# A decoder layer on one core: cross attention in another order, with a new passage into it and new ends behind it

## The reference

```python
x = x + attention(layernorm(x), W_qkv)                     # one head of 128, causal
x = x + cross_attention(layernorm(x), ctx, ctx, mask, ...) # 16 heads of 8, biases on q, k, v and output
x = x + ffn(layernorm(x), w_gate, w_up, w_down)            # 128 -> 384 -> 128, quantised
```

## Time and profile before

| | us |
|---|---|
| median of 3 runs | 374.4 |
| lowest, highest | 369.46, 376.76 |
| profiled execution | 369.51 |
| its span, first to last instruction | 367.7 |

### The profile page before, as it was taken

One profiled execution on the slowest core, in us unless ns is written; L12 is line 12 of the kernel. 1 busy time (PEld: TensorE's weight loads), 2 busy tenths in 40 slices (PEclk: granted clock), 3 DMA queues, 4 the chain that ended last, 5 costly groups with the idle time before them and its releaser, 6 DMA issues.

```text
span 367.7 us, 9555 instructions
## 1 busy us (share of the span) xinstructions
PE 308.6 (84%) x3621; PEld 204.2 (56%) x3621; DVE 282.1 (77%) x589; ACT 248.0 (67%) x452; POOL 177.7 (48%) x321
## 2 busy tenths in 40 slices
PE   3999999997599998989889899689987668660996
PEld 2697877774366665656556566434432223220996
DVE  5369988876767878888887885858779967897563
ACT  3368888875358787778778776268697736991850
POOL 3559999973313474755666471100058841662000
PEclk9999999999759999999999999889998998895699
DMA  5961666665640000000000000000000000000034
GB/s 139 299 193 32 200 206 205 200 206 160 213 133 2 5 2 4 4 3 4 2 4 4 4 4 2 0 0 0 2 0 1 0 0 0 1 0 0 18 98 116
DMA packets 23751, 22.67 MB, mean 62 GB/s; under 512 B 3545, under 2 KB 21402, under 8 KB 23578
## 3 DMA queue, kind: packets, MB, share of 16 engines
q1 hardware_dynamic: 22170, 21.78, 19.5%
q10 hardware_dynamic: 1536, 0.28, 0.4%
HBM read 15.75 MB, written 6.31 MB: 60 GB/s over the span
## 4 chain that ended last, share of the span: by engine, by line
PE 41%; DVE 22%; POOL 17%; issue 8%; ACT 7%; DMA 2%; SPq 1%; ACTq 1%; POOLq 0%; DVEq 0%
DVE mxs L1537 8%; PE banks L834 7%; PE banks L655 7%; PE banks L874 7%; PE banks L616 4%; DVE nm L1331 4%; POOL rstd L352 3%; PE banks L677 3%; POOL X L448 3%; POOL pickd L371 2%; PE banks L673 2%; PE banks L668 2%; PE banks L621 2%; DMA k_dram<-klo 2%; PE banks L536 2%
## 5 line engine op out<-in xcount | busy, mean ns | idle before, releaser
L1331 DVE TENSOR_REDUCE nm<-banks 128x8 f32<-128x1024 f32 x64 | 78.0, 1219 | 21.7 <-PE banks L612 21.7
L1028 ACT ACTIVATE PT<-banks,bmask,vmask 128x1024 f32<-128x1024 f32 x64 | 76.8, 1200 | 2.1 <-PE banks L621 2.1
L834 PE MATMUL banks<-X3T,upT 128*128 128x512 f32 x96 | 48.9, 660 | 15.4 <-DVE mxs L1537 9.4
L484 POOL TENSOR_TENSOR G<-ng,sq 128x1536 int32<-128x1536 int32 (+3 forms) x9 | 26.1, 2903 | 43.6 <-DVE sq L1562 43.6
L1537 DVE TENSOR_REDUCE mxs<-G 128x1 f32<-128x1536 int32 (+4 forms) x27 | 41.9, 1566 | 6.7 <-ACT G L1064 6.7
L655 PE MATMUL banks<-PT,VP 128*32 128x128 f32 x1024 | 43.0, 287 | 0.4
L834 PEld LDWEIGHTS banks<-X3T,upT 128*128 128x128 f32 x96 | 19.1, 208 | 43.4 <-issue 20.6
L908 ACT ACTIVATE h<-X,shift,rstd 128x128 f32<-128x128 f32 x64 | 26.4, 482 | 13.9 <-POOL shift L397 13.8
L655 PEld LDWEIGHTS banks<-PT,VP 128*32 128x32 f32 x1024 | 25.7, 112 | 8.1 <-issue 0.7
L1016 ACT ACTIVATE oT<-banks 128x128 f32<-128x128 f32 x32 | 8.9, 277 | 30.9 <-PE banks L673 30.9
L433 POOL CAST NM<-nm 128x64 bf16<-128x64 f32 x32 | 7.6, 238 | 43.8 <-DVE nm L1331 43.8
(11 more groups left out here) (183 smaller groups left out, 710.8 us busy)
## 6 DMA issues: line engine op xcount, KB each, us to landing
kd<-k_dram SPq DMA_DIRECT2D x32, 128.0 KB, 2.7
qd<-q_dram SPq DMA_DIRECT2D x32, 128.0 KB, 2.5
ctxg<-in_ctx_dram SPq DMA_DIRECT2D x8, 256.0 KB, 3.2
X3T<-m_dram SPq DMA_DIRECT2D x1, 1792.0 KB, 10.1
out_dram<-y SPq DMA_DIRECT2D x7, 256.0 KB, 2.3
X<-in_x_dram SPq DMA_DIRECT2D x3, 512.0 KB, 10.0
k_dram<-khi SPq DMA_DIRECT2D x8, 128.0 KB, 1.8
k_dram<-klo SPq DMA_DIRECT2D x8, 128.0 KB, 2.2
```

The costliest lines, as they stand in the source:

```text
L834: m = pe.matmul(bank(2 + FC * (g % 2) + k), w[:, k * P:k * P + P], grp(X3T, g), start=True, stop=True)
L1028: act.activation(PT[:, a, :], bank(2 + 2 * a, 2), ACT.Exp, bias=bmask[:, n:n + 1], scale=vmask[:, n:n + 1]).then_inc(S["t_exp"], 1)
L1331: V.tensor_reduce(nm[:, n % 2, 2 * NSET * a:2 * NSET * (a + 1)], bank(0, 2).rearrange("p (h m) -> p h m", m=P), AX.X, ALU.max, negate=True ...
```

## The change

- Passage: on TensorE the first scores come first, then the last group's values and keys and the queries of group 6; the rows of group 7 are turned behind scores of sequence 2. ScalarE takes over two copies (`cT`, the values of group 7) from VectorE. The last group's `khi`, `klo` go to the buffer `h`, which is free by then (`k_parts`). The weights' last step (`f_deq`) goes from VectorE to GpSimd. PSUM banks 6 and 7 change roles in the first stage.
- Cross attention: VectorE does `stat3`, `aggregate3` and `largest3` between the two maxima; `largest3` is done in halves, in the third and fourth sequence of a group. On TensorE `project(n - 1)` goes behind `both(n, 1)`.
- End of the cross attention: four groups' copies to X3T go to ScalarE, the copy of upT too; TensorE turns groups 4 and 5 ahead of `turn(31)`; VectorE does `attend(31)` right behind the aggregate.
- ffn: the up scale is made in two steps with a `sigmoid_levels` between, and its transposition goes one `hidden` earlier; GpSimd makes the whole last gate product, in halves; in the last group VectorE reduces group 6 ahead of its own product.

Bank numbers that only change roles, and waits that follow from a move, are left out of the diff.

```diff
--- before.py
+++ after.py
+        def k_parts(g):
+
+            if g == NG - 1:
+                both = h[:, :].bitcast(F16)
+                return both[:, 0:GT], both[:, GT:2 * GT]
+            return khi[:, :], klo[:, :]
 
...
-            pool.wait_ge(S["l_vc"], NG)
+            pool.wait_ge(S["f_quant"], 7)
+            nc.gpsimd.tensor_tensor(R3, R3, bc(blkscale[:, :].unsqueeze(2), wide), ALU.mult).then_inc(S["f_deq"], 1)
+            add_constant(NG - 2)
             pool.wait_ge(S["c_vp"], 1)
...
+                pool.wait_ge(S["l_vc"], n // GB + 1)
...
             maxima_split(0)
             values(0)
+            scale_and_shift(1, NG - 1, "l_agg", "l_h", "l_var", "l_pow", "l_neg", "l_rstd")
             maxima_split(1)
+            add_constant(NG - 1)
...
-            level_product(NG - 1, slice(0, PB), NG + 1)
+            for h_ in range(2):
+                level_product(NG - 1, slice(h_ * PB, (h_ + 1) * PB), NG + 1)
...
-            turn_rows2(NG - 2)
-            weighted_values1(NG - 1)
             pe.wait_ge(S["t_k0"], 64)
             pe.wait_ge(S["t_q0"], 64)
             pe.wait_ge(S["s_exp"], GB * NG)
             pe.wait_ge(S["s_pTc"], NG)
             scores_q(0, 1)
-            queries2(NG - 2)
+            weighted_values1(NG - 1)
+            pe.wait_ge(S["t_max"], 1)
+            scores_q(0, 0)
+            turn_rows2(NG - 2)
             values2(NG - 1)
             keys2(NG - 1)
-            pe.wait_ge(S["t_max"], 1)
-            scores_q(0, 0)
-            turn_rows2(NG - 1)
+            queries2(NG - 2)
             pe.wait_ge(S["t_max"], 2)
             scores_q(1, 1)
-            queries2(NG - 1)
             pe.wait_ge(S["c_inj"], JT + 1)
             max_rows(0)
-            pe.wait_ge(S["t_max"], 3)
-            scores_q(1, 0)
             pe.wait_ge(S["l_vc"], NG)
             pe.wait_ge(S["t_mTc"], 1)
             scores_k(0, 0)
-            pe.wait_ge(S["t_max"], 4)
-            scores_q(2, 1)
+            pe.wait_ge(S["t_max"], 3)
+            scores_q(1, 0)
             pe.wait_ge(S["s_x1"], GB * NG)
             pe.wait_ge(S["l_klo"], NG)
             scores_k(0, 1)
+            pe.wait_ge(S["t_max"], 4)
+            scores_q(2, 1)
+            turn_rows2(NG - 1)
             pe.wait_ge(S["t_max"], 5)
             scores_q(2, 0)
-            pe.wait_ge(S["l_qlo"], NG)
-            pe.wait_ge(S["l_hTc"], NG)
-            pe.wait_ge(S["c_wz"], 5)
+            queries2(NG - 1)
 
...
+                if n == 0:
+                    pe.wait_ge(S["l_hTc"], NG)
+                if n == 1:
+                    pe.wait_ge(S["l_qlo"], NG)
...
                 pv(n, 1)
+                both(n, 1)
                 if n > 0:
                     project(n - 1)
-                both(n, 1)
...
             queries(B - 1)
-            turn_weights3(1, 3)
+            turn_early_rows3(B - 1)
             turn(B - 1)
             project(B - 1)
-            turn_early_rows3(B - 1)
+            turn_weights3(1, 3)
             turn_weights3(2, 4)
             pe.wait_ge(S["u_xd"], GB)
             turn_rows3(5, NG - 2)
             pe.wait_ge(S["u_xd"], 2 * GB)
-            pe.wait_ge(S["u_tc"], 5)
+            pe.wait_ge(S["u_tca"], 3)
             turn_rows3(0, NG - 1)
...
+                if g == 0:
                     over_partitions(3, 1, 0)
                 if g == 2:
                     over_partitions(4, 1, 1)
...
-                wait(act, "l_kst", 32 * g)
-                act.activation(khi[:, :], bank(5), ACT.Identity, bias=bcol[:, 1:2]).then_inc(S["l_khi"], 1)
+                if last(g):
+                    act.wait_ge(S["s_hT"], NG)
+                else:
+                    wait(act, "l_kst", 32 * g)
+                act.activation(k_parts(g)[0], bank(5), ACT.Identity, bias=bcol[:, 1:2]).then_inc(S["l_khi"], 1)
...
                     values_copy1(i - 1)
-                if live(i - 2):
+                if live(i - 2) and i < NG:
                     rows2(i - 2)
+            probs_copy1(NG - 1)
+            act.wait_ge(S["l_cT"], NG)
+            act.wait_ge(S["l_k"], NG - 1)
+            act.wait_ge(S["l_v"], NG - 1)
+            act.activation(cT[:, :], bank(2), ACT.Copy).then_inc(S["l_cTc"], 1)
+            keys_high(NG - 2)
+            rows2(NG - 2)
             keys_high(NG - 1)
-            rows2_copy(NG - 1)
-            queries_high(NG - 1)
+            act.wait_ge(S["l_v"], NG)
+            act.activation(grp(V2, NG - 1), bank(3), ACT.Copy).then_inc(S["l_vc"], 1)
+            rows2_copy(NG - 2)
+            queries_high(NG - 2)
...
             max_copy(0)
             for n in range(B):
                 probs(n, 0)
+                if n == 0:
+                    rows2(NG - 1)
+                    rows2_copy(NG - 1)
...
                 probs(n, 1)
+                if n == B - 1:
+                    rows3_copy(0, 2)
+                    rows3_copy(1, 3)
...
             out_copy(B - 1)
+            rows3_copy(0, 4)
+            rows3_copy(1, 5)
             turn_copy(B - 1)
-            act.wait_ge(S["f_t"], 3)
-            act.activation(downT[:, :], bank(4)[:, 0:FC * P], ACT.Copy).then_inc(S["f_tc"], 1)
-            for n, g in ((5, NG - 2), (0, NG - 1)):
-                act.wait_ge(S["u_t"], g + 1)
-                act.activation(grp(X3T, g), bank(n), ACT.Copy).then_inc(S["u_tca"], 1)
+            for m_, w, n in ((1, upT, 3), (2, downT, 4)):
+                act.wait_ge(S["f_t"], m_ + 1)
+                act.activation(w[:, :], bank(n)[:, 0:FC * P], ACT.Copy).then_inc(S["f_tc"], 1)
+            rows3_copy(5, NG - 2)
+            rows3_copy(0, NG - 1)
 
...
-            context_copy(NG - 1)
+            maxima(0, 0)
             residual1(NG - 1)
+            maxima(0, 1)
             stat2(NG - 1)
-            maxima(0, 0)
             keys_low(NG - 2)
+            maxima(1, 0)
+            keys_low(NG - 1)
+            maxima(1, 1)
             queries_low(NG - 2)
-            values_copy2(NG - 1)
-            maxima(0, 1)
-            keys_low(NG - 1)
-            maxima(1, 0)
-            weight_values()
-            queries_low(NG - 1)
-            maxima(1, 1)
             maxima(2, 0)
             maxima(2, 1)
+            queries_low(NG - 1)
...
-                for k in range(2):
-                    if n + 3 < B:
-                        maxima(n + 3, k)
-                if g > 1 and b == 1:
-                    dve.wait_ge(S["u_x3"], GB * (g - 1))
-                    largest3(g - 2, g - 2, (0, GB))
-                if 1 < n < B:
-                    if n == B - 2:
-                        for k in range(2):
-                            rows3_copy(k, k)
-                    if n < B - 1:
-                        stat3(n - 2)
+                if n + 3 < B:
+                    maxima(n + 3, 0)
+                if n == B - 2:
+                    for k in range(2):
+                        rows3_copy(k, k)
+                if 1 < n < B - 1:
+                    stat3(n - 2)
                 if g > 0 and b == 1:
                     aggregate3(g - 1)
+                if g > 1 and b > 1:
+                    k = b - 2
+                    dve.wait_ge(S["u_x3"], GB * (g - 2) + 2 * k + 2)
+                    largest3(g - 2, 2 * (g - 2) + k, (2 * k, 2 * k + 2))
+                if n + 3 < B:
+                    maxima(n + 3, 1)
...
-            for k in range(2):
-                rows3_copy(k, 2 + k)
-            dve.wait_ge(S["u_xd"], GB)
-            largest3(NG - 2, NG - 2, (0, GB))
-            weights_copy(0, gateT, 2)
             residual(B - 2)
             stat3(B - 2)
             aggregate3_last(0, GB - 1)
             attend(B - 1)
-            weights_copy(1, upT, 3)
+            weights_copy(0, gateT, 2)
+            largest3(NG - 2, 2 * NG - 4, (0, GB))
+            residual(B - 1)
+            stat3(B - 1)
+            aggregate3_last(GB - 1, GB)
             dve.wait_ge(S["u_rstd"], NG)
             for b in range(GB - 1):
                 row3(NG - 1, b)
-            residual(B - 1)
-            stat3(B - 1)
-            aggregate3_last(GB - 1, GB)
-            dve.wait_ge(S["u_xd"], 2 * GB - 1)
-            largest3(NG - 1, NG - 1, (0, GB - 1))
-            for k in range(2):
-                rows3_copy(k, 4 + k)
             dve.wait_ge(S["u_rstd"], NG + 1)
             row3(NG - 1, GB - 1)
             dve.wait_ge(S["u_xd"], 2 * GB)
-            largest3(NG - 1, NG, (GB - 1, GB))
-            dve.wait_ge(S["u_mx"], NG + 1)
+            largest3(NG - 1, 2 * NG - 3, (0, GB))
+            dve.wait_ge(S["u_mx"], 2 * NG - 2)
...
                 sigmoid_levels(g, slice(0, FW), g + 2)
+                if g == NG - 1:
+                    scales_from(2, 3, 0)
...
-                    scales(2, 3, 0)
+                    row_maxima(2, 3)
             g = NG - 1
-            dve.wait_ge(S["b_ng"], NG + 1)
-            dve.wait_ge(S["b_sq"], NG + 1)
```

(23 more changed lines are left out.)

99 lines of the change are left out of this document (56 added, 43 removed).

## The result

| | before | after |
|---|---|---|
| median of 20 runs each, in us | 369.79 | 372.17 |
| lowest, highest | 366.67, 376.76 | 371.05, 373.71 |
| profiled execution, its span | 369.51, 367.7 | 372.69, 370.8 |

The ratio is 1.0078, with a 95% interval from 1.0054 to 1.0102: the change makes the kernel slower, by 0.8%, which is little but clear of the interval. Executions in which a kernel was well above its own fastest time, at a lower mean clock, are left out of the ratios, so a ratio is not quite the quotient of two medians. Most of that miss is in the starting point: before has a median of 369.79 where I took 372.5.

The account below looks back on a forecast made before the run. It took a ring through TensorE, VectorE and ScalarE, all near their limit, to bound each sequence. Terms -2.0 + 10.6 + 0.3 - 2.0 - 2.7 - 0.75 = +3.45 us on 372.5 gave 376 us, range 360 to 384.

Parts of the forecast that it names:

- The base: Whole kernel: starting time of 372.5 us, the mean of four times shown, to which the terms' sum was added.
- Part (c): Cross attention loop: next first products wait for the copy of the moved projection; 4.31 us a sequence, +10.6 us.
- the doubt named last: Cross attention loop: the waits for the maxima and for wo might overlap instead of lying in series, making the whole wrong.
- Part (a): Cross attention loop: statistics and half of largest3 fit VectorE's 0.63 us gap; 0.96 us stalls go, worth about 5.5 us.
- The bound for only one wait: Cross attention loop: if only the wait for the maxima binds, 4.03 us a sequence, or +3.0 us.
- The passage: From the first stage into the loop: L662 of sequence 2 at 104.3 against 106.30, -2.0 us; bounds nothing and -4.
- The dequantisation on GpSimd: Passage: moved to GpSimd, 2.9 to 4.1 us, hidden in its wait of some 5 us for the rows of group 6.
- The end of the cross attention: L662 of sequence 31 to the maximum over rows: attend(31) comes sooner; -2.0 us, between 0 and -3.
- The ffn: Gated part: silu levels sooner by the up scale and last gate product, -2.7 us; idle before L1604 filled, -0.75.
- Neither wait binds: Rival, cross attention loop: every sequence takes 3.74 us, loop -4.8, whole kernel 360 us; chance 0.20.
- Only the first: Rival, cross attention loop: only the wait for the maxima binds, 4.03 us a sequence, whole kernel 368 us; chance 0.15.
- The clock falls in the loop: Rival, cross attention loop: more waiting brings TensorE's lower clock, seven more sequences at 5.4 us, total 384 us; chance 0.20.

Follow-up runs that it names:

- The kernels with one wait less: After, either with wo filled from a constant, not waiting for the projection (361.56 us), or with the first maxima over half the keys (363.61 us).
- projection back: After, with the projection back between the second products and the second scores: 356.59 us, ratio 0.9622.
- short first maxima: After, with the first of a sequence's two maxima looking at half of the keys: 363.61 us, ratio 0.9812.
- old passage: After, with the projection back in its old place and the passage of before: 358.42 us, ratio 0.9664; again 357.91 us, 0.9662.
- the two kernels without the wait for the projection: After, with wo filled from a constant: 361.56 us, ratio 0.9757; the same with first maxima over half the keys too: 359.33 us, 0.9696.

## Why the prediction was right in its parts, and which step failed

**The base failed.** The prediction said: "The mean of the four is 372.5, and 372.5 + 3.5 = 376." The sum of +3.45 nearly stands: +3.1 between the two spans, +3.2 between the two profiled executions, +2.4 between the medians, +2.9 by the ratio. But the four times shown were too few, and two of them (374.4 and 376.76) were high. Over 20 runs the median is 369.79, close to the profiled 369.51 that I had moved away from. So 376 stood 6.2 us above what before really takes, where the kernel lost 2.4 to 2.9. On the right base it is 369.79 + 3.45 = 373.2, which is 1.1 above the measured 372.17.

**Part (c), the projection behind the second scores: right, and the largest term.** Forecast 4.31 us a sequence and +10.6; measured 4.31 or 4.32 and +10.7. The links too: from `queries` to the second scores 2.25 us (162.51 to 164.76; 2.24 forecast), 0.55 to the projection, 0.52 to `wo`, 0.42 for the copy and the way back, 0.57 to the next `queries`. The kernels with one wait less show that both waits are real and lie in series, so the doubt named last, that they might overlap, fell. One reading was off and changed nothing: `wo` was not copied "a whole third of a sequence behind its projection". The projection ends at 165.41 (164.92 + 0.49) and the copy starts at 165.72: 0.31 us.

**Part (a), the statistics between the maxima: right.** The stalls went, and with that edit alone the ratio's 0.9786 is some 8 us (5.4 to 10.5) against "about 5.5 us" forecast; the timelines account for 4.8 of it (105.81 less 27 x 3.74). Statistics (0.28) and half of `largest3` (0.40, not 0.36) overlap a little and take from 164.62 to 165.21, 0.59 us, so they fit the gap of 0.63. In after they cost nothing beside the slower ring: VectorE then stands 0.86 us in front of the reciprocal, waiting for TensorE.

**The bound for only one wait was mis-sized:** 4.03 where the kernel shows 3.84, because I took 0.42 and 0.25 from rows of the old order, the second with a wait for `wo` in it; the new order shows 0.33 and 0.15. It did not enter the sum.

**The passage: -1.9 for -2.0, in part by luck.** L662 of sequence 1 was forecast at 100.2 and that of sequence 2 at 104.3; the first came at 101.88, where it was, the second at 105.64, which is 0.7 us sooner than in before and not 2.0. The timeline shows why: `queries2(NG - 1)` (L622) now stands directly ahead of it and starts at 100.01, and at the lower clock it takes 2.08 us. I had left this instruction out of the path. What gain there is came behind it: sequences 2 and 3 follow after 3.76 and 3.88 us, where before had 4.42 and 5.16. The larger part, 1.28 us, is the step from sequence 2 to 3, and there the granted clock differs, a term that the sum did not have: it was back in before only at about 110.4, in after at about 103.8. The windows of after:

```profile
96.00:110.00 14.00, 11.84 (x206) 7.10 (x206) 10.02 (x11) 9.22 (x17) 4.07 (x13) 0.76 0.50 159
140.00:160.00 20.00, 16.49 (x403) 10.89 (x403) 15.15 (x30) 14.84 (x30) 10.66 (x29) 1.00 0.01 3
```

0.76 in the passage, against 0.53. In other executions of the new passage the clock stayed low longer and sequence 3 came at 111.45 to 113.23, as said above: the agreement within 0.1 us belongs to the two executions compared. That `khi` of group 7 no longer waits for a store was right (90.88, released by TensorE, against 93.69).

**The dequantisation on GpSimd was hidden, and shorter than my bounds** of 2.9 to 4.1 us from 512-column rows. GpSimd's timeline in after:

```profile
82.76 2.13 POOL L426 TENSOR_TENSOR WR<-WR,blkscale 128x1152 f32<-128x1152 f32 x1
...
335.84 1.26 POOL L520 TENSOR_TENSOR G<-ng,X 128x512 int32<-128x512 int32 x1
```

VectorE did the same in 1.35 us in before. The Trainium skill (GPSIMD Engine Reference, Engine selection) has GpSimd about twice as slow as VectorE for operations with two inputs. This pair makes it 1.6; for the 768-column products of the last pass, 1.82 us on GpSimd against 0.96 on VectorE while GpSimd was idle, it is 1.9.

**The end of the cross attention: -2.4 for -2.0.** `on_` of sequence 31 comes 8.7 us behind its `max_rows` (239.66 - 230.95), before 10.6. This edit was not run alone, but the stretch is 13.2 to 13.4 us in all eight profiled executions that have it and 15.5 to 16.0 in the four that do not.

**The ffn: -4.1 for -3.45.** The third stretch gave -2.8, the products' end -1.3 where I had -0.75. The third stretch won since VectorE has the turned maxima of the up scale at 307.17 with no wait, where it stood 2.58 us. What I had not counted is VectorE's last product: 1.21 us instead of 1.91. GpSimd's part of that product, in the timeline of before,

```profile
331.67 1.29 POOL L503 TENSOR_TENSOR G<-ng,X 128x512 int32<-128x512 int32 x1
```

still ran for 0.8 us beside VectorE's, which started at 332.14. In after it runs from 335.84 for 1.26 us and has ended at 337.10, ahead of VectorE's start at 337.21. The kernel with the ffn's edits alone shows the same 1.21. VectorE's smaller products of the same pass bear out that this is the cause, since they lie beside GpSimd's (313.01 to 314.83, 315.82 to 317.65) for different times. The timeline of before, VectorE:

```profile
311.88 0.96 DVE L1604 TENSOR_TENSOR G<-ng,X 128x768 int32<-128x768 int32 x1 [1.38 <-ACT ng L1098]
...
314.14 1.51 DVE L1604 TENSOR_TENSOR G<-ng,X 128x768 int32<-128x768 int32 x1 [1.16 <-ACT ng L1098]
```

With nothing beside it such a product takes 0.96 us, with 0.69 us of GpSimd's beside it 1.51, and the next one, from 317.24, with 0.41 us beside it 1.24. So VectorE's product became longer by about 0.7 to 0.85 of the time for which the two lay side by side.

**The rivals.** *Neither wait binds*: no, 4.31. *Only the first*: no; taken alone each costs. *The clock falls in the loop*: no. With 16.5 of 20 us busy instead of 18.2 the granted clock stayed at 1.00 from 140 to 160, and the low stretch ended earlier than before, not later. The Trainium skill (TensorE: Matmul & The Clock Gate, Part 1) says that activity releases the throttle; the rival read out of it that more waiting could bring the lower level back, and this loop shows no sign of that. What the clock took, it took in the passage, and not alike in all executions. The rival's price was also too low: its 5.16 us were of a sequence that ran at full clock from about 110.4 on. One wholly at the lower level took 5.93, in the kernel with the statistics moved alone.

## What to carry to other kernels

An instruction between two others may be the cover of a wait: before you move it, compare its length with the slack of the wait behind it (0.42 us of projection against 0.17 us of slack), and look at its new place for what waits on its result at once (here the copy of `wo`, 0.42 us with the way back, every sequence). Filling an idle gap of another engine with its own small work was free and worth some 2% (1.4 to 2.8), so the two edits of one loop have to be timed apart. And three or four times are too few for a base when they differ by 2%: take the time of the execution whose trace you add to.

## What the runs showed of the hardware that I had not expected

How long TensorE keeps the lower clock (1.2 GHz) in the passage is not a property of the kernel alone. In the profiled executions it was 6.8 us (after, projection back, short first maxima), 10.2 (old passage), 13.7 (before, and before with the projection moved), 17.1 (ffn alone, and the second profiles of projection back and of old passage), 20.5 (the two kernels without the wait for the projection) and 34.1 us (statistics alone). Two executions of one and the same kernel showed 6.8 and 17.1, two of another 10.2 and 17.1. At that level a sequence takes 5.93 us instead of 3.74. The totals go with the mean clock: of the runs of before beside the experiments, five of the six at mean clocks of 0.913 to 0.922 took 373.6 to 375.7 us, those at 0.939 or more 367.1 to 371.0. Where in the kernel the clock was low in the runs without a trace is not shown. The Trainium skill (TensorE: Matmul & The Clock Gate, Part 1) says of the ramp at a kernel's start that it varies from run to run and costs under 1% of a typical kernel's span; the stretch here lies in the middle of the kernel, and executions of one kernel lie 1 to 2.6% apart along with the clock. Why runs with the new passage keep the higher mean clock was not tried.

Two elementwise products side by side on VectorE and GpSimd are not free: of 0.82 us side by side, VectorE's product of 1024 columns became 0.7 us longer (1.91 for 1.21), and the shorter ones followed the same way (0.96, 1.24 and 1.51 us).
